# Softmax maxima of a head pair: turned first and split behind the transpose, with a reordered second block

## The chip, the cores and the metric

The kernel runs on one core of a Trainium2 chip. The metric is the time of one execution on the device in microseconds (us), median of several runs. One further execution is profiled; durations, waits and stretches below come from that one.

## The reference, cut to what matters

Two blocks of a transformer run one after the other over x of 8 sequences, 512 tokens and 256 features, with 16 heads of 16. The first has a bias on its scores; the second, `_L1_cond_ref`, masks the keys:

```
qkv = (x @ qkv_w).reshape(b, n, 3, H, D)
scores = jnp.einsum('bhnd,bhmd->bhnm', q, k) * scale
scores = jnp.where(mask, scores, -jnp.inf)
attn = jax.nn.softmax(scores, axis=-1)
out = jnp.einsum('bhnm,bhmd->bhnd', attn, v)
attn_out = out @ proj_w + proj_b
x = x + gate_msa[:, None, :] * _modulate(_layernorm(attn_out), shift_msa, scale_msa)
mlp_out = _mlp(x, fc1_w, fc1_b, fc2_w, fc2_b)
x = x + gate_mlp[:, None, :] * _modulate(_layernorm(mlp_out), shift_mlp, scale_mlp)
```

The mask of the second block leaves only keys among the last 128 tokens of each sequence. The kernel finds that out on the chip, from a flag, and then takes a short form of the second block; with these inputs it always does.

## The kernel before

A pass is one sequence in one block: passes 0 to 7 are the first block, 8 to 15 the second (`B` is 8, `N` 16). Each engine has its own program, written out as a loop over passes (`turn`), and waits on semaphores. Products outside the attention are cut into pieces: `v`, `qk` (queries and keys, four), `t1`, `t3`, `t2` (transposes), `wout`, `up` (eight) and `down` (four token tiles of eight chunks each). Pieces share three PSUM banks in a fixed round. While TensorE does the attention of pass n, it does the front of pass n + 1 and the back of pass n - 1 between.

In the short form (`short(n)`) a turn has 12 steps, p = 0 to 11. Tables set which pieces stand where: `HEADS` at the slots k = 3p, 3p + 1, 3p + 2, and `HEADS_DOWN` which of the 32 chunks of `down` stand at a slot. The heads go in 8 pairs, q = 0 to 7. For each pair:

- TensorE, step q + 2: `pair_scores_of` (L905) makes the scores, queries by keys, of both heads into the two `score` banks.
- DVE: `peaks_of` takes the maxima of every query (L1414), 8 columns for 2 heads and 4 token tiles; then a rounded high part (L1419) and the low rest (L1421) into `split_peak`, 16 columns.
- TensorE: `turn_peaks` (L912) transposes these into a corner of score bank 0, 16 rows of 128.
- DVE: `take_peaks` (L1429) copies them negated to `peaks`. The next `pair_scores_of` waits for it, as it overwrites the bank.
- ACT: `load_peaks` (L1113) issues a transfer of `peaks` into four rows of `q_rows` below the query rows, against which `k_rows` holds ones.
- TensorE, step q + 3: `turned_scores_of` (L924) makes the scores again, keys by queries, with the maxima subtracted by the extra rows. It waits for that transfer.
- ACT: `head_exp` (L1107), the exponentials, behind `load_peaks` of the next pair in its program. Then for every four heads, at steps 5, 7, 9, 11: `attend_heads` (L934), ACT's copy of its result (L1127), `heads_to_tokens` (L942), and DVE's division (L1437, L1439).

The order on TensorE within a step is: pair scores, slots 3p and 3p + 1, the values product, turned maxima, turned scores, slot 3p + 2, head outputs to tokens. At step 2 DVE adds the residual of the pass before (`add_tile`, L1268) or, at pass 8, applies the norm (`first_norm`, L1220); the `t2` transposes (L835) wait for it. On SP's queue, a short turn starts with the load of a residual if it is the first, and `load_few` loads the next pass's query and key rows of a group once `turned_scores_of` has used the old ones. ACT's gelu ("hidden", L1072) frees the bank of an `up` piece; gelu and exponential are in different tables, and a change between them costs a table load on ACT.

## Time and profile before

| what | value |
| --- | --- |
| median of 3 runs | 1460.7 us (1453.96 to 1461.02) |
| profiled execution, its own time | 1457.03 us |
| its span, first to last instruction | 1455.2 us |
| mean granted TensorE clock | 0.978 |
| busy: TensorE, DVE, ACT, POOL | 90%, 55%, 53%, 52% |
| second block, first pair scores to last | 900 to 1395 us |
| the eight turns of the second block | 893 to 1405 us, 62 to 66 us each |

Times are us from the first instruction. A granted clock of 1.00 is 2.4 GHz, and 0.5 is 1.2 GHz. "[1.89 <-DVE x_res L1268]" behind an instruction means that its engine sat idle for 1.89 us and that this DVE result released it. In the trace each fp32 chunk of `down` is two matmul records.

### The profile page before, as it was taken

Reading aid. Unit: us, or ns where it says so; the run is one execution under the profiler, and the core shown is the slowest. Engines: PE = TensorE matmul, PEld = TensorE weight load, DVE = VectorE, ACT = ScalarE, POOL = GpSimd, SP = SyncE. Lnnn points to the kernel's source line nnn. Section 1 sums busy time; section 2 is a strip of 40 time slices with the busy share of each in tenths; the row PEclk is TensorE's granted clock in tenths of the full one; section 3 lists DMA queues with packets and bytes.
Section 4 is the critical chain, followed back from the end, with each engine's and each line's share of the span. In section 5 each row is a group of like instructions: output and inputs, shape, how many; then the busy total and the mean of one; then the engine's idle time right before and its main releaser. Section 6 shows DMA issues by size and latency. Waiting matters only on the chain. (4 is left out here: it accounts for less than half of the span.)

```text
span 1455.2 us, 24552 instructions
## 1 busy us (share of the span) xinstructions
PE 1309.6 (90%) x8789; PEld 1004.0 (69%) x8789; DVE 803.2 (55%) x2240; ACT 770.5 (53%) x1262; POOL 757.1 (52%) x939
## 2 busy tenths in 40 slices
PE   4898999999999999999999997989888898988777
PEld 3676777777777777777777775666666666665556
DVE  3766645645646656656645643464655556454452
ACT  3565665665665765665655752544544353453522
POOL 3788876776776776776776761020413222140323
PEclk9999999999999999999999998999999999999988
DMA  8432222223213213213213215353424242433100
GB/s 258 130 127 57 71 84 72 73 75 83 74 64 89 75 58 88 78 55 88 79 54 110 92 41 164 113 152 108 151 67 145 61 155 93 123 116 86 45 2 29
DMA packets 98259, 133.98 MB, mean 92 GB/s; under 512 B 16802, under 2 KB 51498, under 8 KB 98130
## 3 DMA queue, kind: packets, MB, share of 16 engines
q1 hardware_dynamic: 96850, 131.80, 30.3%
q8 instruction: 73, 1.20, 0.3%
q10 hardware_dynamic: 1280, 0.53, 0.2%
q14 instruction: 56, 0.46, 0.1%
HBM read 72.64 MB, written 58.75 MB: 90 GB/s over the span
## 5 line engine op out<-in xcount | busy, mean ns | idle before, releaser
L617 POOL TENSOR_SCALAR shifted<-shifted,row_max 128x512 f32<-128x512 f32 x512 | 360.6, 719 | 220.1 <-DVE row_max L1380 218.2
L1380 DVE CUSTOM_DVE_ANT_0 shifted<-score,bias 128x512 f32<-128x512 f32 x512 | 332.7, 687 | 255.4 <-PE score L855 165.6
L1091 ACT ACTIVATE probs<-turned 128x512 f32<-128x512 f32 x512 | 278.2, 596 | 211.4 <-PE turned L867 209.8
L867 PE MATMUL turned<-ident,shifted 128*128 128x128 f32 x2048 | 270.0, 275 | 6.8 <-POOL shifted L617 6.0
L867 PEld LDWEIGHTS turned<-ident,shifted 128*128 128x128 f32 x2048 | 233.6, 141 | 55.6 <-issue 26.6
L783 PE MATMUL dense<-w_down,hidden 128*128 128x256 f32 x1024 | 253.3, 383 | 0.8 <-ACT hidden L1072 0.8
L610 POOL TENSOR_SCALAR bias<-dist,scale 128x1024 f32<-128x1024 f32 x192 | 220.0, 1146 | 13.6 <-DMA down_bias<-in_L_cond_b 13.6
L855 PE MATMUL score<-k_rows,q_rows 97*128 97x512 f32 x512 | 205.2, 456 | 22.1 <-DVE row_max L1380 10.1
L783 PEld LDWEIGHTS dense<-w_down,hidden 128*128 128x128 f32 x1024 | 185.6, 191 | 32.6 <-issue 9.6
L763 PE MATMUL dense<-feat_m,w_up 128*128 128x512 f32 x768 | 188.4, 400 | 3.5 <-ACT hidden L1072 1.8
L763 PEld LDWEIGHTS dense<-feat_m,w_up 128*128 128x128 f32 x768 | 144.3, 192 | 37.1 <-ACT hidden L1072 5.3
L855 PEld LDWEIGHTS score<-k_rows,q_rows 97*128 97x128 f32 x512 | 92.1, 190 | 65.0 <-DVE row_max L1380 51.5
L882 PE MATMUL pv<-probs,v_ext 128*32 128x256 f32 x2048 | 123.8, 382 | 0.8 <-DVE attn L1405 0.8
L631 POOL CAST mask_colf<-mask_col 128x4 f32<-128x4 uint8 x8 | 1.5, 188 | 234.7 <-PE pv L934 224.8
L1107 ACT ACTIVATE probs<-turned 128x512 f32<-128x512 f32 x128 | 69.5, 595 | 92.7 <-PE turned L924 61.8
L1072 ACT ACTIVATE hidden<-dense,up_bias 128x512 f32<-128x512 f32 x128 | 86.4, 688 | 54.2 <-PE dense L763 53.8
L763 PE MATMUL dense<-feat_a,w_qkv 128*128 128x512 f32 x384 | 109.0, 427 | 2.8 <-DVE feat_a L1334 2.8
L1414 DVE TENSOR_REDUCE row_max<-score 128x8 f32<-128x1024 f32 x64 | 78.1, 1221 | 36.5 <-PE score L905 36.5
L882 PEld LDWEIGHTS pv<-probs,v_ext 128*32 128x32 f32 x2048 | 60.2, 109 | 54.0 <-issue 17.7
L763 PEld LDWEIGHTS dense<-feat_a,w_qkv 128*128 128x128 f32 x384 | 73.7, 204 | 16.9 <-issue 3.2
L1059 ACT ACTIVATE qk_high<-dense 128x512 fp32r<-128x512 f32 x64 | 38.2, 597 | 77.1 <-PE dense L763 77.1
L1080 ACT ACTIVATE bias<-dist,scale 128x1024 f32<-128x1024 f32 x64 | 73.6, 1151 | 0.0
(138 smaller groups left out, 1497.3 us busy)
## 6 DMA issues: line engine op xcount, KB each, us to landing
qk_rows<-qk_high SPq DMA_DIRECT2D x128, 256.0 KB
q_rows<-qk_rows SPq DMA_DIRECT2D x64, 384.0 KB
qk_rows<-qk_low SPq DMA_DIRECT2D x64, 256.0 KB
k_rows<-qk_rows SPq DMA_DIRECT2D x68, 192.0 KB
x_in_t<-in_x SPq DMA_DIRECT2D x8, 512.0 KB, 3.8
x_res<-in_x SPq DMA_DIRECT2D x8, 512.0 KB, 5.5
x_mid<-x_norm SPq DMA_DIRECT2D x8, 512.0 KB, 3.3
x_in_t<-x_mid SPq DMA_DIRECT2D x8, 512.0 KB, 3.9
```

The source lines that it names most:

```text
L610: pool.tensor_scalar(bias[:, u % 2, :, :], dist[:, 2 * half:2 * half + 2, :], scale[:, h:h + 1], 0.0, ALU.mult, ALU.add).then_inc(s["bias_ ...
L617: ins = pool.tensor_scalar(shifted[:, u % 3, i, :], shifted[:, u % 3, i, :], -1.0, row_max[:, t % 6:t % 6 + 1], ALU.mult, ALU.add)
L763: mm = pe.matmul(out_ap, left, right, start=(i == 0), stop=(i == len(terms) - 1))
L783: mm = pe.matmul(bank_of(piece, m)[:, 0:D], hidden[:, c, P * i:P * i + P], w_down[:, c, :], start=(c == 0), stop=(c == FCH - 1))
L855: pe.matmul(score_bank[t % 2], q_rows[0:KROWS, g % 2, j // 2, q0:q0 + P], k_rows[0:KROWS, g % 2, j // 2, j % 2, :], start=True, stop=True) ...
L867: mm = pe.transpose(turned_bank[z % 2][:, HALF * kk + P * i:HALF * kk + P * i + P], shifted[:, u % 3, i, P * kt:P * kt + P], ident[:, :])
L882: mm = pe.matmul(pv_bank[SLOT * j:SLOT * j + SLOT, 0:HALF], v_ext[:, kt, HG * (gq // 2) + j, :], probs[:, (4 * gq + j) % RING, kt, :], sta ...
L1072: act.activation(hidden[:, i, :], bank[:, :], ACT.Gelu_apprx_tanh if m < B else ACT.Gelu, bias=up_bias[:, i:i + 1]).then_inc(used(piece, m ...
L1080: act.activation(bias[:, u % 2, :, :], dist[:, 2 * half:2 * half + 2, :], ACT.Copy, scale=scale[:, h:h + 1]).then_inc(s["act_bias_ready"], 1)
L1091: act.activation(probs[:, u % RING, 2 * pair:2 * pair + 2, :], turned_bank[z % 2][:, :].rearrange("p (a c) -> p a c", a=2), ACT.Exp)\
L1380: dve.tensor_tensor_reduce(shifted[:, u % 3, i, :], score_bank[t % 2], bias[:, u % 2, i, :], 1.0, 3.0e38, ALU.add, ALU.min, row_max[:, t % ...
L1414: dve.tensor_reduce(row_max[:, :].rearrange("p (a t) -> p t a", a=2), pair_scores, mybir.AxisListType.X, ALU.max).then_inc(s["peak_ready"], 1)
```

## The change

`split_peak` is gone. The 8 columns of maxima are transposed as they are (`turn_peaks` reads `row_max`), and DVE splits them behind the transpose: the high part negated and rounded, then in a second operation the rest, both reading the bank. ACT issues one transfer for the high rows when they are there (`peak_high`) and one for the low rows (`peaks_ready`); `peaks_loaded` counts 32 a pair. The rows in `q_rows` are ordered by part and then by head. On TensorE, the turned scores of the pair before now stand ahead of the turned maxima. On DVE, the residual's adds (or the norm at pass 8) at step 2 stand ahead of the pieces of that step's first slot. `HEADS_DOWN` moves chunks from slots 17, 20 and 26 to the slots ahead of them. The load of the first block's last residual moves on SP from the first short turn to the end of the turn before, ahead of the load of that turn's last group.

```diff
--- before.py
+++ after.py
@@ -70,8 +70,8 @@
              10: [("up", 0), ("up", 1), ("up", 2), ("up", 3)], 13: [("up", 4), ("up", 5), ("up", 6), ("up", 7)],
              19: [("down", 0)], 23: [("down", 1)], 28: [("down", 2)], 35: [("down", 3)]}
     HEAD_STEPS = H // 2 + 4
-    HEADS_DOWN = {16: (0, 4), 17: (4, 6), 19: (6, 9), 20: (9, 11), 22: (11, 14), 23: (14, 16), 25: (16, 19),
-                  26: (19, 21), 28: (21, 24), 29: (24, 25), 31: (25, 28), 34: (28, 29), 35: (29, 32)}
+    HEADS_DOWN = {16: (0, 6), 19: (6, 10), 20: (10, 11), 22: (11, 14), 23: (14, 16), 25: (16, 20), 26: (20, 21),
+                  28: (21, 24), 29: (24, 25), 31: (25, 28), 34: (28, 29), 35: (29, 32)}
 
     ANY = {0: [("v", 0), ("v", 1)], 1: [("t3", 0), ("t3", 1)], 2: [("v", 2), ("v", 3)], 3: [("t1", 0), ("t1", 1)],
            4: [("wout", 0)], 5: [("wout", 1)], 6: [("wout", 2)], 7: [("wout", 3)], 9: [("qk", 0)],
@@ -192,8 +192,7 @@
         hidden = sb("hidden", [P, FCH, L])
         feat_tmp = hidden[:, FCH - DC:FCH, :]
         row_max = sb("row_max", [P, 2 * TT])
-        split_peak = sb("split_peak", [P, 4 * TT], F32R)
-        peaks = sb("peaks", [4 * TT, P], F32R)
+        peaks = sb("peaks", [2 * TT, 2, P], F32R)
         minus_mean = sb("minus_mean", [P, TT])
         norm_shift = sb("norm_shift", [P, TT])
         stats = sb("stats", [P, 2, TT, 6])
@@ -245,7 +244,7 @@
                  "stats_ready0", "stats_ready1", "mean_ready0", "mean_ready1", "var_ready0", "var_ready1",
                  "rstd_ready0", "rstd_ready1", "norm_ready0", "norm_ready1", "bias_added", "mid_ready",
                  "res_ready0", "res_ready1", "scaled", "y_ready", "y_stored", "scale_step", "row_ones", "peak_high",
-                 "split_ready", "peak_turned", "peaks_ready", "peaks_loaded", "mean_minus", "norm_shift_ready", "normed",
+                 "peak_turned", "peaks_ready", "peaks_loaded", "mean_minus", "norm_shift_ready", "normed",
                  "y_scaled", "y_done", "last_ready", "tile_stats0", "tile_stats1", "tile_mean0", "tile_mean1", "tile_var0",
                  "tile_var1", "tile_rstd0", "tile_rstd1")
         s = {name: sem(name) for name in names}
@@ -467,7 +466,7 @@
                 sp.dma_start(flags, early_flag[:, :]).then_inc(s["flag_stored"], 16)
                 for a in range(2):
                     for x in range(2):
-                        at = PEAK_AT + 2 * a + x
+                        at = PEAK_AT + a + 2 * x
                         sp.dma_start(k_rows[at:at + 1, :, :, a, :].bitcast(F32),
                                      q_rows[MASK_AT:KROWS, 0:2, :, :].bitcast(F32)).then_inc(s["row_ones"], 16)
 
@@ -475,8 +474,6 @@
                 sp.wait_ge(s["halves_stored1"], STORED * (n + 1))
                 sp.sem_inc(s["base_free"], 1)
                 if n == B:
-                    sp.wait_ge(s["y_ready"], B - 1)
-                    load_res(B - 1)
                     sp.wait_ge(s["scores_used"], TILES * B)
                     load(raw_out[1], d["L1_cond_proj_w"].rearrange("(c p) n -> p c n", p=P), "wout_loaded")
                     load(raw_up[1], d["L1_cond_fc1_w"].rearrange("(c p) n -> p c n", p=P), "wup_loaded")
@@ -527,7 +524,8 @@
                     if n == 1:
                         sp.wait_ge(s["mod_stored"], 16)
                         sp.wait_ge(s["row_ones"], 64)
-                    load_res(n - 1)
+                    if n != B:
+                        load_res(n - 1)
                     if n - 1 >= B:
                         load_mod(n - 1)
                 if n == B - 1:
@@ -552,6 +550,9 @@
                     load_group(n + 1, 0)
                     if n > 0:
                         store_y(n - 1)
+                    if n == B - 1:
+
+                        load_res(n)
                     load_group(n + 1, 1)
                     return
                 if n + 1 < N:
@@ -908,8 +909,8 @@
                 mm.then_inc(s["scores_ready"], 2 * TT)
 
             def turn_peaks(n, q):
-                pe.wait_ge(s["split_ready"], H // 2 * (n - B) + q + 1)
-                pe.transpose(score_bank[0][0:4 * TT, 0:P], split_peak[:, :].bitcast(F32), ident[:, :])\
+                pe.wait_ge(s["peak_ready"], H // 2 * (n - B) + q + 1)
+                pe.transpose(score_bank[0][0:2 * TT, 0:P], row_max[:, :], ident[:, :])\
                     .then_inc(s["peak_turned"], 1)
 
             def turned_scores_of(n, q):
@@ -917,7 +918,7 @@
                 g, pair = q // 2, q % 2
                 if n == B and q == 0:
                     pe.wait_ge(s["row_ones"], 64)
-                pe.wait_ge(s["peaks_loaded"], 16 * (H // 2 * (n - B) + q + 1))
+                pe.wait_ge(s["peaks_loaded"], 32 * (H // 2 * (n - B) + q + 1))
                 for a in range(2):
                     h = 2 * q + a
                     pe.wait_ge(s["probs_ready"], TILES * n + (TT * (h - 1) if n > B or h > 0 else 0))
@@ -985,10 +986,10 @@
                                 down_chunks(n - 1, *HEADS_DOWN[k])
                         if attended:
                             attend_heads(n, (p - 5) // 2)
+                        if 3 <= p < 3 + H // 2:
+                            turned_scores_of(n, p - 3)
                         if 2 <= p < 2 + H // 2:
                             turn_peaks(n, p - 2)
-                        if 3 <= p < 3 + H // 2:
-                            turned_scores_of(n, p - 3)
                         for piece, m in pieces(HEADS, 3 * p + 2, n):
                             dense(piece, m)
                         if 3 * p + 2 in HEADS_DOWN:
@@ -1109,9 +1110,10 @@
 
             def load_peaks(n, q):
                 g, pair = q // 2, q % 2
-                act.wait_ge(s["peaks_ready"], H // 2 * (n - B) + q + 1)
-                act.dma_start(q_rows[PEAK_AT:ALL_ROWS, g, pair, :].bitcast(F32), peaks[:, :].bitcast(F32))\
-                    .then_inc(s["peaks_loaded"], 16)
+                for x, made in enumerate(("peak_high", "peaks_ready")):
+                    act.wait_ge(s[made], H // 2 * (n - B) + q + 1)
+                    act.dma_start(q_rows[PEAK_AT + 2 * x:PEAK_AT + 2 * x + 2, g, pair, :].bitcast(F32),
+                                  peaks[:, x, :].bitcast(F32)).then_inc(s["peaks_loaded"], 16)
 
             def normalize(m):
                 act.wait_ge(s["norm_shift_ready"], m - B + 1)
@@ -1409,25 +1411,20 @@
 
             def peaks_of(n, q):
 
-                count = H // 2 * (n - B) + q + 1
                 dve.wait_ge(s["scores_ready"], TILES * n + 2 * TT * (q + 1))
                 dve.tensor_reduce(row_max[:, :].rearrange("p (a t) -> p t a", a=2), pair_scores,
                                   mybir.AxisListType.X, ALU.max).then_inc(s["peak_ready"], 1)
-                dve.wait_ge(s["peak_ready"], count)
-                peak = row_max[:, :].rearrange("p (a t) -> p a t", a=2)
-                parts = split_peak[:, :].rearrange("p (a x t) -> p a x t", a=2, x=2)
-                dve.tensor_copy(parts[:, :, 0, :], peak).then_inc(s["peak_high"], 1)
-                dve.wait_ge(s["peak_high"], count)
-                dve.tensor_tensor(parts[:, :, 1, :], peak, parts[:, :, 0, :].bitcast(F32), ALU.subtract)\
-                    .then_inc(s["split_ready"], 1)
 
             def take_peaks(n, q):
                 count = H // 2 * (n - B) + q
                 dve.wait_ge(s["peak_turned"], count + 1)
                 if count > 0:
-                    dve.wait_ge(s["peaks_loaded"], 16 * count)
-                dve.tensor_scalar(peaks[:, :], score_bank[0][0:4 * TT, 0:P], -1.0, None, ALU.mult)\
-                    .then_inc(s["peaks_ready"], 1)
+                    dve.wait_ge(s["peaks_loaded"], 32 * count)
+                turned = score_bank[0][0:2 * TT, 0:P]
+                dve.tensor_scalar(peaks[:, 0, :], turned, -1.0, None, ALU.mult).then_inc(s["peak_high"], 1)
+                dve.wait_ge(s["peak_high"], count + 1)
+                dve.scalar_tensor_tensor(out=peaks[:, 1, :], in0=turned, scalar=-1.0, in1=peaks[:, 0, :].bitcast(F32),
+                                         op0=ALU.mult, op1=ALU.subtract).then_inc(s["peaks_ready"], 1)
 
             def divide_heads(n, g):
                 dve.wait_ge(s["token_ready"], GQ * n + 2 * g + 2)
@@ -1491,14 +1488,14 @@
             def turn(n):
                 if short(n):
                     for p in range(HEAD_STEPS):
-                        for piece, m in pieces(HEADS, 3 * p, n):
-                            dense(piece, m)
                         if p == 2:
                             if n == B:
                                 first_norm("norm", 1, n - 1)
                             else:
                                 for t in range(TT):
                                     add_tile(n - 1, 0, t)
+                        for piece, m in pieces(HEADS, 3 * p, n):
+                            dense(piece, m)
                         if 2 <= p < 2 + H // 2:
                             peaks_of(n, p - 2)
                         for piece, m in pieces(HEADS, 3 * p + 1, n):
```

TensorE at steps 3 to 5 of pass 9, from the turned maxima of pair 1 on, before:

```order
L912 MATMUL score<-ident,split_peak 16x128
L924 MATMUL turned<-q_rows,k_rows 128x512 x2
L905 MATMUL score<-k_rows,q_rows 128x256 x4
L763 MATMUL dense<-feat_m,w_up 128x512 x24
L912 MATMUL score<-ident,split_peak 16x128
L924 MATMUL turned<-q_rows,k_rows 128x512 x2
L905 MATMUL score<-k_rows,q_rows 128x256 x4
L783 MATMUL dense<-w_down,hidden 128x256 x4
L934 MATMUL pv<-probs,v_ext 32x512 x4
L912 MATMUL score<-ident,split_peak 16x128
L924 MATMUL turned<-q_rows,k_rows 128x512 x2
L783 MATMUL dense<-w_down,hidden 128x256 x2
```

and now:

```order
L925 MATMUL turned<-q_rows,k_rows 128x512 x2
L913 MATMUL score<-ident,row_max 8x128
L906 MATMUL score<-k_rows,q_rows 128x256 x4
L764 MATMUL dense<-feat_m,w_up 128x512 x24
L925 MATMUL turned<-q_rows,k_rows 128x512 x2
L913 MATMUL score<-ident,row_max 8x128
L906 MATMUL score<-k_rows,q_rows 128x256 x4
L784 MATMUL dense<-w_down,hidden 128x256 x6
L935 MATMUL pv<-probs,v_ext 32x512 x4
L925 MATMUL turned<-q_rows,k_rows 128x512 x2
L913 MATMUL score<-ident,row_max 8x128
```

The turned scores (`turned`) stand ahead of the turned maxima (the transpose into `score`), which now stand right ahead of the next pair scores; all six chunks of `down` stand ahead of the values product (`pv<-probs,v_ext`).

TensorE at steps 9 to 11 of the same pass, around the turned maxima of the last pair, before:

```order
L905 MATMUL score<-k_rows,q_rows 128x256 x4
L783 MATMUL dense<-w_down,hidden 128x256 x3
L934 MATMUL pv<-probs,v_ext 32x512 x4
L912 MATMUL score<-ident,split_peak 16x128
L924 MATMUL turned<-q_rows,k_rows 128x512 x2
L783 MATMUL dense<-w_down,hidden 128x256
L942 MATMUL pv<-ident,head_out 128x128 x4
L783 MATMUL dense<-w_down,hidden 128x256 x3
L924 MATMUL turned<-q_rows,k_rows 128x512 x2
L783 MATMUL dense<-w_down,hidden 128x256
L934 MATMUL pv<-probs,v_ext 32x512 x4
```

and now:

```order
L784 MATMUL dense<-w_down,hidden 128x256 x3
L935 MATMUL pv<-probs,v_ext 32x512 x4
L925 MATMUL turned<-q_rows,k_rows 128x512 x2
L913 MATMUL score<-ident,row_max 8x128
L784 MATMUL dense<-w_down,hidden 128x256
L943 MATMUL pv<-ident,head_out 128x128 x4
L784 MATMUL dense<-w_down,hidden 128x256 x3
L925 MATMUL turned<-q_rows,k_rows 128x512 x2
L784 MATMUL dense<-w_down,hidden 128x256
L935 MATMUL pv<-probs,v_ext 32x512 x4
```

Between the last turned maxima and the last turned scores, the turned scores of pair 6 no longer stand.

DVE at step 2 of the same pass, before:

```order
L1341 SCALAR_TENSOR_TENSOR qk_low<-dense,qk_high 128x512 x3
L1268 SCALAR_TENSOR_TENSOR shifted<-dist,rstd,shifted 128x256 x4
L1414 TENSOR_REDUCE row_max<-score 128x4x2
L1419 CAST split_peak<-row_max 128x2x4
L1421 TENSOR_TENSOR split_peak<-row_max,split_peak 128x2x4
L1337 TENSOR_TENSOR feat_m<-dense,feat_m 128x512 x2
L1429 TENSOR_SCALAR peaks<-score 16x128
L1341 SCALAR_TENSOR_TENSOR qk_low<-dense,qk_high 128x512
```

and now:

```order
L1343 SCALAR_TENSOR_TENSOR qk_low<-dense,qk_high 128x512 x2
L1270 SCALAR_TENSOR_TENSOR shifted<-dist,rstd,shifted 128x256 x4
L1343 SCALAR_TENSOR_TENSOR qk_low<-dense,qk_high 128x512
L1415 TENSOR_REDUCE row_max<-score 128x4x2
L1339 TENSOR_TENSOR feat_m<-dense,feat_m 128x512 x2
L1424 TENSOR_SCALAR peaks<-score 8x128
L1426 SCALAR_TENSOR_TENSOR peaks<-score,peaks 8x128
L1343 SCALAR_TENSOR_TENSOR qk_low<-dense,qk_high 128x512
```

The four adds of the residual (`shifted<-dist,rstd,shifted`) stand ahead of the third low part of queries and keys; cast and subtraction of the maxima are gone, and a second operation on `peaks` follows the first.

## Rows read from the trace of the kernel before

**Rows 1.** Stretches of us: busy PE, PEld, DVE, ACT, POOL; granted clock, DMA share, GB/s.

```profile
956.00:1019.00 63.00, 54.63 (x297) 40.67 (x296) 35.85 (x78) 29.08 (x44) 9.25 (x13) 1.00 0.51 151
...
1149.00:1213.00 64.00, 56.15 (x296) 41.70 (x296) 35.40 (x82) 29.64 (x47) 16.18 (x19) 0.97 0.36 115
```

**Rows 2.** Time line of TensorE, pass 9 then 12: start, us, instruction, [idle before].

```profile
973.93 1.64 PE L763 MATMUL dense<-feat_a,w_qkv 128*128 128x512 f32 x6
...
1164.17 1.98 PE L835 MATMUL dense<-ident,x_res 128*128 128x128 f32 x8 [1.89 <-DVE x_res L1268]
1166.81 0.38 PE L912 MATMUL score<-ident,split_peak 128*16 128x128 f32 x1 [0.66 <-DVE split_peak L1421]
1166.84 2.71 PE L763 MATMUL dense<-feat_a,w_qkv 128*128 128x512 f32 x6
...
1175.36 0.27 PE L912 MATMUL score<-ident,split_peak 128*16 128x128 f32 x1
...
1176.09 0.71 PE L905 MATMUL score<-k_rows,q_rows 97*128 97x256 f32 x4
...
1181.17 1.67 PE L763 MATMUL dense<-feat_m,w_up 128*128 128x512 f32 x6 [0.22 <-ACT hidden L1072]
1182.68 0.27 PE L912 MATMUL score<-ident,split_peak 128*16 128x128 f32 x1
...
1186.65 1.06 PE L934 MATMUL pv<-probs,v_ext 128*32 128x512 f32 x8 [0.86 <-ACT probs L1107]
...
1189.71 0.72 PE L905 MATMUL score<-k_rows,q_rows 97*128 97x256 f32 x4
...
1192.43 0.28 PE L912 MATMUL score<-ident,split_peak 128*16 128x128 f32 x1 [0.70 <-DVE split_peak L1421]
...
1193.75 0.83 PE L905 MATMUL score<-k_rows,q_rows 97*128 97x256 f32 x4
...
1202.00 0.28 PE L912 MATMUL score<-ident,split_peak 128*16 128x128 f32 x1 [0.99 <-DVE split_peak L1421]
...
1203.31 0.81 PE L905 MATMUL score<-k_rows,q_rows 97*128 97x256 f32 x4
...
1206.35 0.28 PE L912 MATMUL score<-ident,split_peak 128*16 128x128 f32 x1
...
1209.00 0.82 PE L924 MATMUL turned<-q_rows,k_rows 101*128 101x512 f32 x2
...
1210.84 1.06 PE L934 MATMUL pv<-probs,v_ext 128*32 128x512 f32 x8 [0.59 <-ACT probs L1107]
```

**Rows 3.** Time line of DVE, the same turn of pass 12.

```profile
1162.94 0.69 DVE L1341 SCALAR_TENSOR_TENSOR qk_low<-dense,qk_high 128x512 fp32r<-128x512 f32 x1 [0.97 <-ACT qk_high L1059]
1163.55 1.66 DVE L1268 SCALAR_TENSOR_TENSOR x_res<-dist,rstd,x_res 128x256 f32<-128x256 f32 x4
1165.13 1.22 DVE L1414 TENSOR_REDUCE row_max<-score 128x8 f32<-128x1024 f32 x1
...
1197.23 0.28 DVE L1429 TENSOR_SCALAR peaks<-score 16x128 fp32r<-16x128 f32 x1 [0.99 <-DMA q_rows<-peaks]
...
1206.67 0.28 DVE L1429 TENSOR_SCALAR peaks<-score 16x128 fp32r<-16x128 f32 x1
```

**Rows 4.** Time line of ACT and its queue (ACTq), the same turn.

```profile
1183.30 0.64 ACTq L1113 DMA_DIRECT2D q_rows<-peaks  x1
...
1185.31 1.08 ACT L1107 ACTIVATE probs<-turned 128x512 f32<-128x512 f32 x2
...
1193.41 0.64 ACTq L1113 DMA_DIRECT2D q_rows<-peaks  x1
...
1206.98 0.64 ACTq L1113 DMA_DIRECT2D q_rows<-peaks  x1
```

**Rows 5.** Time line of TensorE at the entry of the second block.

```profile
895.31 1.02 PE L763 MATMUL dense<-w_out,feat_m 128*128 128x256 f32 x6 [2.12 <-DVE x_res L1350]
```

**Rows 6.** DMA issues by line: count, KB each, median us to landing.

```profile
x_res<-in_x SPq DMA_DIRECT2D x8, 512.0 KB, 5.5
```

## The prediction

> **What bounds the kernel now.** I read the granted clock by stretches first, then the time line of TensorE over one turn of the second block (a turn is one sequence: 16 heads in 8 pairs), and last the lines of the engines that TensorE waits for. The change touches only the eight turns of the second block (about 893 to 1405 us) and one load ahead of them. A turn takes some 64 us, in which TensorE has work in 56 [rows 1]: it sets the pace, and what counts is which waits of TensorE go and come. In the turn shown [rows 2] it waits 1.89 us for the residual rows (DVE L1268), 0.66 for the maxima of pair 0, 0.22 at the last "up" piece (for ACT), 0.86 at the first product with the values (for ACT's exponentials), 0.70 and 0.99 for the maxima of pairs 4 and 6, and 0.59 before the last heads. The reader should see that ahead of pairs 1 to 3 nothing waits for maxima: the order of before hides them behind the "up" products. I call the turning of a pair's maxima (L912) T, and the scores matmuls of the next pair (L905) S.
>
> **Costs that the rows give.** From T to the DVE's take of the turned maxima 0.32, which itself takes 0.28, and 0.63 from T to ACT's issue of the transfer [rows 2, 3, 4]. An issue holds ACT for 0.64 us, and the exponentials start behind it: 2.63 behind T where the table must be loaded (1182.68 to 1185.31) [rows 2, 4]. The turned scores of pair 7 run 2.02 us behind the issue without a wait (1206.98 to 1209.00), so a transfer is usable by then; beside SP's loads it took 3.82 (1193.41 to 1197.23) [rows 2, 3, 4].
>
> **1. The move of the adds on DVE (step 2).** DVE idles 0.97 before the low half of a query/key piece, does it, and only then adds the residual (4 tiles in 1.66) [rows 3]. Now the adds come first, and TensorE's wait for them shrinks by about 1.6 of 1.89. The reduce starts about 0.95 earlier. Cast and subtraction are gone between reduce and T: before, T stood 1.68 behind the reduce's start (1165.13 to 1166.81), of which 1.22 is the reduce; now about 1.27 [rows 2, 3]. So T of pair 0 comes 1.35 earlier. S of pair 1 gains less: the DVE still does the two low halves of the norm first (about 1.3 us), then both takes; S is ready at about 1167.35. With a full clock the piece between takes 1.64 (pass 9), so S would have come at 1168.3 [rows 2]. **Gain 0.9 a turn.**
>
> **2. The order of T and the turned scores, and the second take.** The turned scores of the pair before (0.54 us of TensorE's time) now stand ahead of T. Behind T, S overwrites the bank, so it waits for both takes: 0.32 + 0.28, a step of 0.03, and a second operation of the same 128 columns, taken at 0.28, make 0.95 with the release. For pairs 1 and 2 nothing stands between T and S. Before it was 0.73 from T to S (1175.36 to 1176.09), with the turned scores inside [rows 2]; now it is 0.54 + 0.95 = 1.5. **Loss 0.8 at pair 1.** Pair 2 has the same, but there ACT's lateness covers it, as follows.
>
> **3. The second issue on ACT.** ACT still issues the maxima of pair q before it takes the exponentials of pair q - 1. T is 0.55 later, and the second issue takes 0.64 more, so exponentials and what follows them come 1.2 later seen from the turned scores. At pair 1 the "hidden" activations follow and free the bank of the last "up" piece, at which TensorE already waits [rows 2, 4]. Seen from pair 1 that piece is 1.2 later, of which 0.8 was counted: **loss 0.4.** At pair 2, T is 0.55 later and the exponentials another 0.64; the first values product stood 3.97 behind T (1182.68 to 1186.65) and now stands about 4.6, so **loss 1.2**, S's wait of 0.85 and the two down chunks moved ahead of it (step 16 now has six, step 17 none) lying in that same time. What hides them is ACT; were ACT faster, they would stand there themselves.
>
> **4. Pairs 3 to 6.** From the values product to S of pair 4 it was 3.06 (1186.65 to 1189.71). Now it is 1.0 + 0.54 + 0.95 = 2.5, as the two chunks are already done: **gain 0.55.** The waits of 0.70 and 0.99 for maxima go, since the chunks and the turned scores (some 2.9 us) cover the reduce; but with one chunk left in steps 20 and 26, S waits about 0.45 behind T, and the values products of steps 7 and 9 wait 0.2 for the later exponentials. From S to S I get 3.95 instead of 4.04 (1189.71 to 1193.75), 0.1 more for the next and 0.4 less for the third: **gain 0.4** [rows 2].
>
> **5. Pair 7.** Its turned scores stood 2.65 behind T (1206.35 to 1209.00), without a wait [rows 2]. Now only one chunk, the turning of head outputs and three chunks lie between, about 2.1, and the second transfer is issued at 1.27 behind T. I take 1.8 for it to be usable, a little under the 2.02 that bounds it from above: it arrives at 3.1 to 3.2, and TensorE waits 1.0. From S of pair 7 to the last values product it was 7.53 (1203.31 to 1210.84). Now T comes at 4.0 (3.04 as before, 0.2 for later exponentials, 0.2 for the turned scores of pair 6 and these themselves 0.54), the turned scores 3.15 later, and the product 1.84 behind them as before: 9.0, **loss 1.5**. The Trainium skill, "DMA: Bandwidth & Descriptors", section "Anatomy of one DMA", gives a fixed cost of about 2.0 us a transfer whatever its size (a fit for another issuing path); by that the last wait would be 1.2 and the sum 1.6 us higher over eight turns. Two small transfers in place of one save nothing there by that rule, and the row of 2.02 leaves room for it.
>
> **The sum.** A steady turn: -0.9 + 0.8 + 0.4 + 1.2 - 0.55 - 0.4 + 1.5 = +2.05. Six of them: +12.3. The last turn has no query/key pieces, so step 1 gives 0.1 instead of 0.9: +2.9. The first turn waits for the norm's rstd and not for the moved piece, and takes 0.3 more for the second take: +3.2; but the load of the residual is now issued before the block, ahead of the last group. Before, it held DVE and so TensorE for 2.12 us [rows 5]; it lands 5.5 behind its issue [rows 6], which moves ahead of that group's load and of the branch, so I take the wait as gone whole, and TensorE is 2.1 earlier: +1.1. The group load that it puts back by one issue on SP is first used at pair 2 of the block, and nothing waits for SP here. Cast and subtraction also free DVE of about 0.4 us a pair, hidden beside TensorE but for what is counted. Sum +16 us on the profiled 1457.0: 1473. The median of the three runs is 3.7 above the profiled execution (they lie at 1454.0 and twice near 1461), so a median would come at 1473 to 1476.7; I give **1475**.
>
> Bounds of the unknown prices: the second take from nothing to 0.69 (a whole 512-column operation [rows 3]); the second issue from nothing to 0.64; the landing from its issue alone, 0.64, to 3.82. They move a turn by -2.1 to +2.
>
> **Rivals.**
> - **The second issue costs ACT nothing** (not slower). If ACT's queue takes both issues in the time of one, TensorE loses 0.6 less at pair 1, 0.3 at pair 2, 0.2 at each of the two values products, and 0.64 at pair 7: 2 us a turn, and with eight turns 1457. For it: the issue can run beside an activation. Against it: the exponentials start right behind the issue's end in every row [rows 4]. It decides from the point at which exponentials start less than 2.8 us behind T with a table load.
> - **The clock pays it back.** The turn shown has a granted clock of 0.97 where pass 9 has 1.00, and the piece behind T of pair 0 takes 2.71 instead of 1.64, so some 1.1 us is lost to a stretch at 1.2 GHz behind the 1.89 and 0.66 of waiting [rows 1, 2]. If such a stretch vanishes from each of the eight turns, 9 us come back: 1464. Against it: new waits of the same size arise at pairs 2 and 7. The Trainium skill, "TensorE: Matmul & The Clock Gate", says in "What's actually happening" that the gate follows how busy the array has recently been; by that alone the place of the stretches moves with the waits, either way.
> - **The second transfer lands late beside SP's loads.** Pairs 2, 4 and 6 are issued with SP's group loads, and now within a third of a microsecond after them. If the second needs 3.82 from its own issue, the turned scores of these pairs wait 0.5 to 0.9 more each: about 1.8 a turn, 1486. I take only 0.2, since the delay looks like one backlog that both stand behind.
> - All gains at once, with no stall behind T: about 1445.
>
> **Chances.** Forecast 0.55, issue 0.12, clock 0.15, late landing 0.13, all gains 0.05. The range takes in the first four with their bounds: 1456 to 1488. Runs can tell about 0.5 per cent. Faster by more than that 0.08 (the last, and part of the clock), within it 0.20 (issue, half of the clock), slower 0.72.
>
> **What would show it.** TensorE idle before S of pairs 2 and 3, released by the new DVE take, some 0.9 us each; none before T of pairs 4 and 6; before the residual's transposes about 0.3 instead of 1.89; two ACT issues of 0.64 in a row; turned scores of pair 7 waiting 1 us; no 2.12 at the entry. The forecast is wrong if S follows T by under 0.8 us at pairs 1 and 2, or if the turn, from values transposes to the next, is not longer than before.

## The result, and the profile after

| | before | changed |
| --- | --- | --- |
| median, 9 runs each | 1460.7 us (1453.96 to 1462.6) | 1467.72 us (1464.27 to 1472.03) |
| ratio, 95% interval | 1 | 1.0056 (1.004 to 1.0072) |
| profiled execution, its own time | 1457.03 us | 1464.27 us |
| span, mean granted clock | 1455.2 us, 0.978 | 1462.5 us, 0.985 |

The change is slower by 0.56%, about half of what was forecast (1475). Stretches of the changed kernel, columns as in [rows 1]:

```profile
956.00:1019.00 63.00, 53.76 (x279) 39.39 (x281) 33.77 (x69) 27.38 (x43) 7.66 (x11) 0.97 0.48 143
1019.00:1083.00 64.00, 55.52 (x294) 40.29 (x294) 32.68 (x74) 28.89 (x47) 16.16 (x19) 1.00 0.37 114
1149.00:1213.00 64.00, 54.85 (x292) 39.54 (x290) 32.68 (x74) 28.49 (x46) 16.14 (x19) 1.00 0.37 115
```

From 1019 us to 1343 every such stretch has a granted clock of 1.00 (2.4 GHz), where before each had 0.97, as the second of [rows 1]. The first one goes the other way, 1.00 before and 0.97 now: pass 9 holds a stretch at half clock that it did not have. TensorE lost time to waits and got some back from the clock. The time line of TensorE in pass 12, answering to [rows 2] (T is L913 here, S L906, turned scores L925):

```profile
1165.35 1.86 PE L836 MATMUL dense<-ident,x_res 128*128 128x128 f32 x8 [0.24 <-DVE x_res L1270]
1168.18 0.27 PE L913 MATMUL score<-ident,row_max 128*8 128x128 f32 x1 [0.97 <-DVE row_max L1415]
1168.20 1.63 PE L764 MATMUL dense<-feat_a,w_qkv 128*128 128x512 f32 x6
1169.87 0.74 PE L906 MATMUL score<-k_rows,q_rows 97*128 97x256 f32 x4
...
1176.55 0.27 PE L913 MATMUL score<-ident,row_max 128*8 128x128 f32 x1
1177.60 0.71 PE L906 MATMUL score<-k_rows,q_rows 97*128 97x256 f32 x4 [0.78 <-DVE peaks L1426]
...
1183.76 1.67 PE L764 MATMUL dense<-feat_m,w_up 128*128 128x512 f32 x6 [1.32 <-ACT hidden L1073]
...
1185.78 0.28 PE L913 MATMUL score<-ident,row_max 128*8 128x128 f32 x1
1186.74 0.74 PE L906 MATMUL score<-k_rows,q_rows 97*128 97x256 f32 x4 [0.68 <-DVE peaks L1426]
1187.32 2.75 PE L784 MATMUL dense<-w_down,hidden 128*128 128x256 f32 x12
1190.40 1.07 PE L935 MATMUL pv<-probs,v_ext 128*32 128x512 f32 x8 [0.33 <-ACT probs L1108]
1192.17 0.70 PE L925 MATMUL turned<-q_rows,k_rows 101*128 101x512 f32 x2 [0.71 <-issue]
...
1193.76 0.71 PE L906 MATMUL score<-k_rows,q_rows 97*128 97x256 f32 x4 [0.34 <-DVE peaks L1426]
...
1201.25 0.70 PE L925 MATMUL turned<-q_rows,k_rows 101*128 101x512 f32 x2 [0.52 <-issue]
...
1206.85 0.74 PE L906 MATMUL score<-k_rows,q_rows 97*128 97x256 f32 x4 [0.25 <-DVE peaks L1426]
...
1210.70 0.28 PE L913 MATMUL score<-ident,row_max 128*8 128x128 f32 x1
...
1213.76 0.71 PE L925 MATMUL turned<-q_rows,k_rows 101*128 101x512 f32 x2 [0.61 <-DMA q_rows<-peaks]
...
1215.49 1.07 PE L935 MATMUL pv<-probs,v_ext 128*32 128x512 f32 x8 [0.59 <-ACT probs L1108]
```

The residual's wait went from 1.89 to 0.24, the one ahead of T of pair 0 from 0.66 to 0.97, the waits of 0.70 and 0.99 for maxima are gone, and the piece behind T of pair 0 takes 1.63 instead of 2.71. New are the waits of S for DVE's second operation (0.78, 0.68, 0.34, 0.25), 1.32 instead of 0.22 at the last "up" piece, and 0.61 before the turned scores of pair 7. Of the 0.71 and 0.52 ahead of the turned scores of pairs 2 and 4 the forecast had almost nothing. DVE (compare [rows 3]) takes twice behind T:

```profile
1164.72 1.66 DVE L1270 SCALAR_TENSOR_TENSOR x_res<-dist,rstd,x_res 128x256 f32<-128x256 f32 x4
...
1166.91 1.22 DVE L1415 TENSOR_REDUCE row_max<-score 128x8 f32<-128x1024 f32 x1
...
1176.86 0.28 DVE L1424 TENSOR_SCALAR peaks<-score 8x128 fp32r<-8x128 f32 x1 [3.55 <-PE score L913]
...
1177.18 0.28 DVE L1426 SCALAR_TENSOR_TENSOR peaks<-score,peaks 8x128 fp32r<-8x128 f32 x1
```

ACT and its queue (compare [rows 4]) show two issues in a row and the exponentials behind both:

```profile
1177.17 2.04 ACTq L1115 DMA_DIRECT2D q_rows<-peaks  x2
1179.33 1.28 ACT L1108 ACT_TABLE_LOAD   x1 [2.49 <-issue]
...
1186.40 1.28 ACTq L1115 DMA_DIRECT2D q_rows<-peaks  x2
1187.77 1.28 ACT L1108 ACT_TABLE_LOAD   x1 [1.61 <-issue]
1189.06 1.09 ACT L1108 ACTIVATE probs<-turned 128x512 f32<-128x512 f32 x2
```

For pair 2 the exponentials start 3.28 behind T (1185.78 to 1189.06), where it was 2.63. At the entry of the block the wait of [rows 5] is gone, and the queries and keys run at the full clock; first the changed kernel, then before:

```profile
891.51 3.07 PE L764 MATMUL dense<-w_out,feat_m 128*128 128x256 f32 x24
894.42 2.96 PE L764 MATMUL dense<-feat_a,w_qkv 128*128 128x512 f32 x12
```

```profile
896.13 4.49 PE L763 MATMUL dense<-feat_a,w_qkv 128*128 128x512 f32 x12
```

**A turn in six stretches.** T of pair q is the turning of its maxima, S of pair q are its scores matmuls. One turn is not enough to compare by. I took the start times of six events of TensorE from the time line in each of the six steady turns (passes 9 to 14): the turn's first transposes (`dense<-ident,attn`), S of pairs 1 and 2, the first values product, S of pairs 4 and 7, the last values product. Means in us; from the last one to the next turn it is 4.62 everywhere. The kernels are those of the experiments below. Each has one profile, so how far these means scatter from run to run is not known.

| kernel | ratio | to S 1 | to S 2 | to 1st values | to S 4 | to S 7 | to last values | turn |
| --- | --- | --- | --- | --- | --- | --- | --- | --- |
| before | 1 | 17.33 | 6.80 | 10.54 | 3.85 | 13.71 | 7.78 | 64.62 |
| changed | 1.0056 | 15.56 | 7.73 | 12.36 | 3.16 | 13.12 | 8.97 | 65.52 |
| forecast, difference | | -0.9 | +0.8 | +1.6 | -0.55 | -0.4 | +1.5 | +2.05 |
| measured, difference | | -1.77 | +0.93 | +1.82 | -0.69 | -0.59 | +1.19 | +0.90 |
| e1 | 0.9978 | 17.63 | 7.14 | 10.56 | 3.40 | 13.73 | 7.86 | 64.93 |
| e2 | 0.9987 | 15.81 | 6.83 | 10.54 | 5.18 | 13.73 | 7.90 | 64.61 |
| e3 | 0.9929 | 16.29 | 7.27 | 11.00 | 3.46 | 13.07 | 8.16 | 63.88 |
| e4 | 1.002 | 15.75 | 7.25 | 12.11 | 4.71 | 13.24 | 8.22 | 65.89 |
| e5 | 1.0042 | 15.89 | 7.38 | 12.62 | 2.49 | 13.27 | 8.98 | 65.26 |
| e6 | 0.9871 | 15.73 | 7.19 | 11.02 | 2.30 | 12.65 | 8.30 | 61.79 |
| e7 | 1.0029 | 15.80 | 7.65 | 12.18 | 2.62 | 13.15 | 9.10 | 65.11 |
| e8 | 1.01 | 16.91 | 7.56 | 12.31 | 2.69 | 13.19 | 9.26 | 66.53 |
| e9 | 0.9965 | 16.39 | 7.42 | 12.12 | 2.38 | 12.65 | 8.32 | 63.90 |
| e10 | 0.9888 | 15.96 | 6.96 | 10.54 | 2.80 | 13.67 | 7.92 | 62.46 |
| e11 | 0.9858 | 16.30 | 7.32 | 10.44 | 2.30 | 12.57 | 8.22 | 61.76 |
| e12 | 1.0041 | 15.80 | 7.67 | 10.75 | 4.48 | 13.80 | 8.85 | 65.96 |

The six turns one by one are 63.27, 63.87, 66.51, 63.76, 64.33, 66.00 before and 66.60, 64.70, 66.28, 65.57, 63.76, 66.21 now. Two of them are shorter than before, and 3.33 of the 5.4 us that all six are longer lie in pass 9. (The first turn takes 70.74 before and the last 60.99, so the "62 to 66 us each" in the table of the kernel before is too narrow.)

In before, passes 10, 12 and 13 run the piece behind T of pair 0 partly at half clock (2.91, 2.71 and 2.89 for the six matmuls), and pair 2 does not wait for its transfer. Passes 11 and 14 run the piece at full clock (1.65) and wait 1.23 and 1.01 at pair 2. Pass 9 has neither; its first stretch is 0.7 longer than in these two. e3 alternates in the same way: half clock in passes 9, 11 and 13, waits of 2.04, 2.47 and 1.90 at pair 2 in 10, 12 and 14. So it is the turn with a short first stretch that meets the wait at pair 2. My reading, argued and not tested by itself, is that its maxima are issued closer behind SP's loads.

### The profile page after: what moved, and what is told of

Same layout as the page of the kernel before. It is cut to its first block and busy times, and to the rows that moved or that the text cites. A ratio compares the mean times of both kernels' runs of the same rounds, so it can differ in the third digit from the quotient of the medians.

```text
span 1462.5 us, 24552 instructions
## 1 busy us (share of the span) xinstructions
PE 1308.8 (89%) x8789; PEld 995.2 (68%) x8789; DVE 787.5 (54%) x2176; ACT 769.6 (53%) x1262; POOL 754.6 (52%) x939
## 5 line engine op out<-in xcount | busy, mean ns | idle before, releaser
L784 PE MATMUL dense<-w_down,hidden 128*128 128x256 f32 x1024 | 250.2, 381 | 0.8 <-ACT hidden L1073 0.8
L784 PEld LDWEIGHTS dense<-w_down,hidden 128*128 128x128 f32 x1024 | 182.2, 190 | 33.1 <-issue 9.6
L764 PE MATMUL dense<-feat_a,w_qkv 128*128 128x512 f32 x384 | 104.3, 413 | 2.8 <-DVE feat_a L1336 2.8
L1424 DVE TENSOR_SCALAR peaks<-score 8x128 fp32r<-8x128 f32 x64 | 17.8, 278 | 147.1 <-PE score L913 147.1
```

Source lines behind the costliest of these rows:

```text
L764: mm = pe.matmul(out_ap, left, right, start=(i == 0), stop=(i == len(terms) - 1))
L784: mm = pe.matmul(bank_of(piece, m)[:, 0:D], hidden[:, c, P * i:P * i + P], w_down[:, c, :], start=(c == 0), stop=(c == FCH - 1))
```

## Experiments: the parts alone

Ratios are to the kernel before, run again beside each kernel, with 95% intervals.

**e1: the early load alone.** The load of the first block's last residual moves as in the change.

> The kernel before with the load of the first block's last residual issued one turn earlier on SP, nothing else. Theory (each wait of TensorE counts for itself): the wait of 2.1 us at the entry of the second block goes, ratio about 0.9985. Rival (clock): the stretches at half clock at the entry go as well, 3 to 4 us in all, ratio 0.9975. If it were hidden elsewhere: 1.000.

1455.74 us, 0.9978 (0.996 to 0.9996): about 3 us, the size of the 2.12 of [rows 5] and what it brings. The interval takes in the wait alone (0.9985) and the wait with its half clock (0.9975); in the profile the first turn is 4.45 shorter (70.74 to 66.29), which speaks for the second.

**e2: and the adds first on DVE.**

```diff
                     for p in range(HEAD_STEPS):
-                        for piece, m in pieces(HEADS, 3 * p, n):
-                            dense(piece, m)
                         if p == 2:
...
+                        for piece, m in pieces(HEADS, 3 * p, n):
+                            dense(piece, m)
```

> As e1, and DVE adds the residual ahead of the query/key piece at step 2. Theory of waits alone: 0.9 to 1.3 us less in each of six turns beyond e1, ratio about 0.993 to 0.994 with e1's part. Rival (clock pays as well): the half-clock stretch behind that wait, 1.1 to 1.7 us in five turns, goes too, the granted clock of passes 10 to 14 reads 1.00, and the ratio is about 0.989.

1456.33 us, 0.9987 (0.9971 to 1.0003): nothing more than e1, where the two theories had 0.993 to 0.994 and 0.989. The table shows where it went. Up to S of pair 1 a turn is 1.82 us shorter than in e1 (17.63 to 15.81), and from the first values product to S of pair 4 it is 1.78 longer (3.40 to 5.18). TensorE in e2, pass 12, at T of pair 0 and at the turned scores of pair 2:

```profile
1164.41 0.28 PE L913 MATMUL score<-ident,split_peak 128*16 128x128 f32 x1 [1.38 <-DVE split_peak L1422]
...
1186.04 1.19 PE L925 MATMUL turned<-q_rows,k_rows 101*128 101x512 f32 x2 [1.58 <-issue]
```

The turned scores of pair 2 wait 1.58 for the maxima and then run at half the clock (1.19 for two matmuls, 0.70 elsewhere). Before has this in two of its six turns; its pass 11, which I had not read, on TensorE, and the issues ahead of it on ACT and on SP:

```profile
1121.60 1.19 PE L924 MATMUL turned<-q_rows,k_rows 101*128 101x512 f32 x2 [1.23 <-issue]
```

```profile
1115.74 0.64 ACTq L1113 DMA_DIRECT2D q_rows<-peaks  x1
```

```profile
1111.96 0.51 SPq L340 DMA_DIRECT2D x_res<-x_mid  x1
1112.51 1.58 SPq L343 DMA_DIRECT2D dist<-mod_rows  x1
```

5.86 us from issue to use: SP's two loads of 512 KB each were issued 3.8 and 3.2 us ahead of it.

**e3: the new order on TensorE and the chunk table too, with the old split and one transfer.** Against the changed kernel this takes back the split alone:

```diff
-                pe.wait_ge(s["peak_ready"], H // 2 * (n - B) + q + 1)
-                pe.transpose(score_bank[0][0:2 * TT, 0:P], row_max[:, :], ident[:, :])\
+                pe.wait_ge(s["split_ready"], H // 2 * (n - B) + q + 1)
+                pe.transpose(score_bank[0][0:4 * TT, 0:P], split_peak[:, :].bitcast(F32), ident[:, :])\
...
-                for x, made in enumerate(("peak_high", "peaks_ready")):
...
+                act.wait_ge(s["peaks_ready"], H // 2 * (n - B) + q + 1)
+                act.dma_start(q_rows[PEAK_AT:ALL_ROWS, g, pair, :].bitcast(F32), peaks[:, :].bitcast(F32))\
+                    .then_inc(s["peaks_loaded"], 16)
```

> The changed kernel with the old split: cast and subtraction ahead of the transpose, one take, one transfer; load, adds, TensorE order and chunk table as changed. Theory (second take and second issue are what costs): against the changed kernel TensorE's waits before the pair scores shrink from 0.7 to 0.8 to some 0.4, ACT's exponentials come 0.9 earlier seen from the turned maxima, and pair 7 waits 0.3 less or more: 1.5 to 2 us a turn, so 12 to 16 us less than the changed kernel, ratio to before about 0.995 to 0.997. Rival (the TensorE order itself costs): little changes against the changed kernel, ratio 1.003 to 1.006.

1449.19 us, 0.9929 (0.9904 to 0.9953): faster than before, and than the 0.995 to 0.997 that I expected. All of the loss, and more, is in the split with its two transfers: 1.27% of the time of before.

**e4: that split with the old order and the old table.**

```diff
-    HEADS_DOWN = {16: (0, 6), 19: (6, 10), 20: (10, 11), 22: (11, 14), 23: (14, 16), 25: (16, 20), 26: (20, 21),
+    HEADS_DOWN = {16: (0, 4), 17: (4, 6), 19: (6, 9), 20: (9, 11), 22: (11, 14), 23: (14, 16), 25: (16, 19),
...
-                        if 3 <= p < 3 + H // 2:
-                            turned_scores_of(n, p - 3)
                         if 2 <= p < 2 + H // 2:
                             turn_peaks(n, p - 2)
+                        if 3 <= p < 3 + H // 2:
+                            turned_scores_of(n, p - 3)
```

> The changed kernel with the old TensorE order (turned maxima ahead of the turned scores) and the old chunk table; split behind the transpose, two transfers, load and adds as changed. Theory: against e2 the waits of 0.7 and 1.0 before the maxima of pairs 4 and 6 shrink by 0.4 each, and 0.25 at pairs 1 and 2, 0.3 at ACT and 0.5 at pair 7 are lost: within 2 us a turn of nothing, ratio to e2 0.998 to 1.003. Rival (split is what costs): as slow as the changed kernel, 1.005.

1461.32 us, 1.002 (1.0004 to 1.0037). The parts don't add up. The split with its two transfers costs 0.33% over e2 in the old order and 1.27% over e3 in the new one; the new order gains 0.58% with one transfer and loses 0.36% with two. It puts T behind the turned scores and leaves less work between T of pair 7 and its use: time that a second issue needs. The last stretch of the table is 8.22 here and 8.97 in the changed kernel. That is part of an answer only. The fourth stretch goes the other way (4.71 here, 3.16 there), so that the steady turns are no shorter here (65.89 and 65.52), and the eight turns take 524.6 us in both profiles. The profiles don't show where the 0.36% lies.

**e8: the changed kernel with the adds behind the piece again,** the edit of e2 undone.

> The changed kernel with DVE's adds again behind the query/key piece. Theory: TensorE waits 1.9 us for the residual again, T of pair 0 comes 0.95 later, and the half-clock stretch returns in most turns: 1 to 2 us a turn, ratio to before 1.010 to 1.014. Rival (the gain is eaten at pair 2's landing, as e2 against e1): ratio 1.005 to 1.007.

1472.37 us, 1.01 (1.0082 to 1.0117). Here the move of the adds is worth 0.44%, some 6 us, while alone (e2) it was worth nothing. In the changed kernel pair 2's maxima are issued later in the turn and meet less of SP's loads: the adds take 1.35 off the first stretch (16.91 to 15.56) and put 0.47 on the fourth (2.69 to 3.16), where in e2 they put 1.78.

## Experiments: what makes the second transfer dear

**e5: e3 with its one transfer issued as two.** DVE's work and all orders are as in e3.

```diff
-                act.dma_start(q_rows[PEAK_AT:ALL_ROWS, g, pair, :].bitcast(F32), peaks[:, :].bitcast(F32))\
-                    .then_inc(s["peaks_loaded"], 16)
+                for a in range(2):
+                    act.dma_start(q_rows[PEAK_AT + 2 * a:PEAK_AT + 2 * a + 2, g, pair, :].bitcast(F32),
+                                  peaks[2 * TT * a:2 * TT * a + 2 * TT, :].bitcast(F32)).then_inc(s["peaks_loaded"], 16)
```

> e3 (old split, new order) with its one transfer of the maxima issued as two, one per head; DVE and TensorE unchanged. Theory (the second issue of 0.64 us on ACT is the main price of the change): exponentials 0.64 later in every pair, TensorE later at the last up piece, at the first values product and before pair 7's turned scores, 1 to 1.5 us a turn, 8 to 12 us, ratio to before 0.999 to 1.001. Rival (the second take ahead of the pair scores is the price): within 3 us of e3, ratio 0.993 to 0.995.

1465.05 us, 1.0042 (1.0029 to 1.0055): 1.13% over e3, about 16 us for 64 further issues of 4 KB, where I expected 8 to 12. That is nearly all that lies between e3 and the changed kernel; the move of the split behind the transpose costs what is left, 0.14%, which the intervals don't tell from nothing.

The Trainium skill, "DMA: Bandwidth & Descriptors", section "Rules for kernel authors", says of two transfers to disjoint partition halves "Don't bother", since both use the same DMA engines. The runs agree that nothing is won, with 16 us as the price here; they show no cost of shared DMA engines, only that of the second issue and of its landing.

**e9: e3 with work on ACT in the place of the second issue.**

```diff
                     .then_inc(s["peaks_loaded"], 16)
+                for i in range(3):
+                    act.activation(idle_out[:, i, :], ident[:, 0:80], ACT.Copy)
```

> The version with the old split and one transfer (e3), with three copies of 80 columns on ACT behind each issue, into a tensor that nothing reads; they take ACT's time and touch no queue, as a second issue would take 0.64 us there. If the second issue costs what it does because ACT takes the exponentials and all behind them later (theory one), this loses what the two issues of e5 lost against e3, some 2 us a turn: ratio to before 1.003 to 1.005. If it costs because the turned scores wait for the later of two transfers (theory two), this loses nothing: 0.991 to 0.995. Between the two, the share of ACT's time can be read off.

1453.16 us, 0.9965 (0.9952 to 0.9977): 0.36% over e3, a third of what the issue costs, and the intervals of e3 and e9 touch. ACT of e9, then of e5, at pair 1 of pass 12:

```profile
1173.19 0.66 ACTq L1115 DMA_DIRECT2D q_rows<-peaks  x1
1173.90 0.59 ACT L1118 ACTIVATE idle_out<-ident 128x80 bf16<-128x80 f32 x3 [0.91 <-DVE peaks L1433]
1174.50 1.28 ACT L1109 ACT_TABLE_LOAD   x1
```

```profile
1178.75 1.28 ACTq L1115 DMA_DIRECT2D q_rows<-peaks  x2
1180.13 1.28 ACT L1108 ACT_TABLE_LOAD   x1 [1.59 <-issue]
```

Both put the table load about 0.6 us back. In the third stretch e9 loses 1.12 a turn against e3 and e5 1.62; over the first three stretches together both lose about 1.35. What differs most is the end of the turn, where the turned scores of pair 7 wait for their transfer: e9 +0.16, e5 +0.82. On the other side both win about 1 us in the fourth stretch (3.46 to 2.38 and 2.49); I put that down to the later issue, with which pair 2 is past SP's loads. The sum over a steady turn is nothing for e9 (63.88 to 63.90) and +1.38 for e5. So neither theory alone: ACT's time is the larger part of the loss up to the first values product and is paid back at pair 2, and the landing of the second transfer at pair 7 is not. What e9 costs in its profile lies outside the steady turns, 2.24 of it in the first turn (67.80 to 70.04) and 2.0 ahead of the block, where the profiles scatter as much.

**e12: the changed kernel with the exponentials ahead of both issues.**

```diff
-                        if 2 <= p < 2 + H // 2:
-                            load_peaks(n, p - 2)
                         if 3 <= p < 3 + H // 2:
                             for a in range(2):
                                 head_exp(n, 2 * (p - 3) + a)
+                        if 2 <= p < 2 + H // 2:
+                            load_peaks(n, p - 2)
```

> The changed kernel, with ACT taking the exponentials of the pair before ahead of both issues of a pair's maxima. The maxima wait for the issues, and the exponentials no longer do. If the price of the second issue is that exponentials and gelu stand 0.64 us further back (the waits of 1.3 us at the last up piece and 0.3 to 0.7 at the values products), those waits go back to what the one-transfer version shows and the ratio to before comes to 0.996 to 1.000. If it is the later landing of the second transfer, the turned scores now wait for it at most pairs and the ratio is 1.006 to 1.015. The filler run says a third of the price is ACT's time, by which I would expect about 1.001 if the transfers had slack.

1462.65 us, 1.0041 (1.0023 to 1.0059), which the intervals don't tell from the changed kernel's 1.0056; I expected about 1.001. The wait of 1.32 at the last "up" piece is gone and the third stretch 1.61 shorter; the fourth is 1.32 longer and the fifth 0.68. TensorE, pass 12:

```profile
1182.27 0.74 PE L906 MATMUL score<-k_rows,q_rows 97*128 97x256 f32 x4 [0.69 <-DVE peaks L1426]
...
1188.77 1.09 PE L925 MATMUL turned<-q_rows,k_rows 101*128 101x512 f32 x2 [2.17 <-issue]
...
1199.25 0.71 PE L925 MATMUL turned<-q_rows,k_rows 101*128 101x512 f32 x2 [1.00 <-issue]
```

What was saved at ACT is waited for at the next landing. I read it so: the waits stand in a row along one path, from T over DVE, ACT's queue and the transfer to the turned scores, beside SP's loads.

## Experiments: SP's loads out of the way

**e6: e3 with the two loads of 512 KB for the residual moved, in passes 9 to 14, behind the turn's last load of query and key rows.**

```diff
-                load_res(n)
-                load_mod(n)
+                late = B < n < N - 1
+                if not late:
+                    load_res(n)
+                    load_mod(n)
...
+                if late:
+                    load_res(n)
+                    load_mod(n)
```

> e3 with SP's loads of residual and modulation rows (1 MB) of passes 9 to 14 moved behind the last group load of the turn. Theory (pair 2's maxima stand behind these loads on the DMA engines, and TensorE then waits up to 2.5 us for them, which eats what the earlier adds gave): that wait is under 0.7 and 1.5 to 2 us a turn go, 9 to 12 us, ratio about 0.985 to 0.987. Rival (the group's own load holds them): no change against e3, ratio 0.993.

1439.68 us, 0.9871 (0.9855 to 0.9887), 0.6% faster than e3. In e3, pass 12, the turned scores of pair 2 wait; SP's issues ahead of them stand below:

```profile
1181.79 0.71 PE L925 MATMUL turned<-q_rows,k_rows 101*128 101x512 f32 x2 [2.47 <-issue]
```

```profile
1171.15 0.51 SPq L340 DMA_DIRECT2D shifted<-x_mid  x1
1171.70 1.47 SPq L343 DMA_DIRECT2D shifted<-mod_rows  x1
```

They were issued 3 us ahead of T of pair 2 (1174.28). In e6 the same pair does not wait, and the loads are issued 28 us behind its T (1174.15):

```profile
1179.13 0.73 PE L930 MATMUL turned<-q_rows,k_rows 101*128 101x512 f32 x2
```

```profile
1202.11 0.45 SPq L340 DMA_DIRECT2D shifted<-x_mid  x1
1202.61 0.49 SPq L343 DMA_DIRECT2D shifted<-mod_rows  x1
```

The fourth stretch is 2.30 in all six turns, and the granted clock is 1.00 in them, as here in pass 12 (columns as in [rows 1]):

```profile
1146.00:1208.00 62.00, 55.30 (x295) 40.32 (x296) 35.23 (x84) 29.98 (x48) 16.53 (x20) 1.00 0.38 121
```

**e7: the same move in the changed kernel.**

> The changed kernel with the same move of the loads. Theory: TensorE waits 0.6 to 0.8 for pair 2's maxima in the changed kernel, so 0.5 to 0.8 us a turn go, 3 to 5 us, ratio about 1.002 to 1.004. Rival (other waits take it): 1.0056 as the changed kernel.

1462.26 us, 1.0029 (1.0017 to 1.004). So the price of the new split with two transfers is no smaller without the two bulk loads: e7 over e6 is 1.6%, where the changed kernel over e3 is 1.27%, a difference within the intervals. The second transfer landing late beside these loads is not the main cost. The rival of the prediction spoke of SP's group loads (query and key rows), which stay where they are. Beside them the turned scores of pair 4 wait 0.18 to 0.79 in e7, and 0.24 to 0.66 in e6 with one transfer: the second adds little there too.

**e10: e2 with the same move,** old order, table and split.

> The kernel before with the early load of the residual, the adds first on DVE (as e2), and SP's large loads of passes 9 to 14 moved behind the turn's last load of query and key rows; the order on TensorE, the split and the single transfer as before. Theory: the adds gained nothing in e2 because the transfer of pair 2's maxima then stood behind those loads; with them away the gain of some 0.4 to 0.6 per cent appears, ratio 0.990 to 0.994, and what remains to e6 (0.987) is the order on TensorE with the chunk table. Rival: the gain was eaten at the turned maxima of pair 0 alone, which stay late here: 0.996 to 1.000.

1443.11 us, 0.9888 (0.9871 to 0.9905): 1% faster than e2, and the fourth stretch is back at 2.80. That confirms where the adds' gain had gone. It is a little more than I expected; the half clock at pair 2 goes with the wait. The move of the loads alone, without the adds, was not run.

**e11: e6 with the exponentials first,** the edit of e12.

> The best version so far (e6) with ACT taking the exponentials of the pair before ahead of the issue of a pair's maxima instead of behind it. Exponentials start up to 0.7 us earlier, the transfer up to 1.1 us later. If the exponentials bound the step (the waits at the values products and at the last up piece), it gains 0.3 to 0.6 us a turn: ratio 0.983 to 0.986. If the landing of the maxima bounds it, the turned scores wait for it at every pair: slower than e6 by 2 us a turn or more, 0.995 to 1.01.

1437.33 us, 0.9858 (0.9841 to 0.9875): the fastest, though not told from e6. The third stretch is 0.58 shorter. With one transfer and the bulk loads moved the later issue costs nothing, unlike in e12.

## Why the prediction was right, and its size too large

The sign, the range and the mechanism held: S waits for both takes, the exponentials stand behind two issues, pair 7 waits for its second transfer, and no wait is left before T of pairs 4 and 6. That the time lies in the range says little by itself, since 1456 to 1488 took in three rivals as well; the forecast's own 1475 was 14 us over before, and 7 were measured. By its steps, in us a steady turn:

- **Step 1, forecast -0.9, measured -1.77. This is the term that was mis-sized.** I reckoned the gain against a full clock ("S would have come at 1168.3"), while S stood at 1169.39. In passes 10, 12 and 13 of before, the stretch from the residual's transposes to S of pair 1 took 5.38, 5.22 and 5.36, in 9, 11 and 14 it took 4.15: 3.5 us over six turns for a half clock. In the changed kernel it is 4.52 in five of six. I had set this apart as the rival "The clock pays it back" with 0.15, and held against it that new waits of the same size arise. They arose, and the granted clock stayed at 1.00 in passes 10 to 14, while pass 9 fell to 0.97: part of that rival came true beside the forecast. The clock is only about half of the excess. Between turns at full clock on both sides the stretch went from 16.62 (passes 11 and 14 of before) to 15.33, a gain of 1.29: the residual's wait shrank by 1.65 as reckoned, and S of pair 1 came 0.3 earlier than the 1167.35 at which I had it ready (1169.87 in a turn that begins 2.84 later).
- **Step 2, +0.8, measured +0.93.** S follows T by 1.05 (1176.55 to 1177.60) where 0.95 was taken; DVE's second operation took 0.28 as taken.
- **Step 3, +1.6, measured +1.82.** The threshold of the rival that the issue costs nothing was 2.8 from T to the exponentials; it was 3.28. e9, +1.12 in this stretch, shows that time on ACT does most of this. The two issues of pair 1 took 1.88 to 2.04 in passes 10 to 12, where the stretch is 12.6 to 12.8, and 1.30 to 1.38 in the others, where it is 12.0 to 12.1 as forecast; that is the excess.
- **Step 4, -0.95 in both stretches, measured -1.28, but not for the reason given.** In turns without a landing wait the fourth stretch went from 2.80 to 2.62 only. Most of the mean's gain is that before lost 3 us there in passes 11 and 14 (5.81 and 5.68), to pair 2's landing. Pass 12, the turn I had read, shows none of that. In the changed kernel it lost up to 1.2.
- **Step 5, +1.5, measured +1.19.** Pair 7 waited 0.61, not 1.0. T to the turned scores was 3.06 (1210.70 to 1213.76); I had put the landing at 3.1 to 3.2, so that was right, and TensorE had 2.45 to do between and not the 2.1 that I took. From the second issue, 1.27 behind T, to the matmul that it released it is 1.79, as I took it and a little below the fixed cost of about 2.0 cited in the prediction. The wait of 0.61 lies below the 1.0 and the 1.2 that these gave.
- **The first turn, +1.1, measured -2.5** (70.74 to 68.25). The entry wait of 2.12 went as said; the half clock behind it went too (4.49 to 2.96 for the same twelve matmuls).
- **The last turn, +2.9, measured +2.3** (60.99 to 63.27).

The sum inside the eight turns is 6 x 0.90 - 2.5 + 2.3 = +5.2, where I had 16. Of the 11 us that are missing, 5.2 are step 1 in six turns and 3.6 the first turn. The profiled execution is 7.2 longer; the other 2 us lie outside the turns. The first block, in which nothing is changed but that load at its end, ends 1.4 later, and over all profiles its end scatters from 886.4 to 892.2 (e1). The medians differ by 7.0.

The traces hold more on how a transfer of ACT's queue is held up: its packets (20 for 8 KB) have a queue of their own. In us behind the issue:

| transfer | first packet | last packet | use |
| --- | --- | --- | --- |
| before, pass 12, pair 7: no other packets | 1.28 | 1.44 | 2.02 |
| e6, pass 12, pair 2: bulk loads moved, group load beside it | 2.29 | 2.57 | 4.36 |
| before, pass 11, pair 2 | 2.93 | 4.95 | 5.86 |
| e3, pass 12, pair 2 | 4.33 | 6.17 | 6.89 |

In e3, SP's queue moved 697 packets between the issue and the first of these 20, with the DMA engines busy throughout (the packets' time comes to 102.5% of 16 engines'). So most of the delay lies ahead of the first packet (3.0 of 4.9 us against pair 7), the rest between the packets, which take 1.8 us instead of 0.2. What stays open is why: the traces don't show whether the transfer stood ready in its queue meanwhile.

## What to carry to other kernels

A small transfer on the way from one engine to another costs its issue on the issuing engine, in front of everything queued there, and its landing. Count both, and don't make two transfers of one. Read several turns of a loop before costing one: the wait that matters can be in every third (here in passes 11 and 14 of six). When an edit on the path gains nothing, look for a wait that grew by the same amount further on: here it was a transfer behind another queue's bulk loads. Moving those gained 0.6 to 1.0% in the kernels with one transfer (e6, e10), more than the whole change cost, and 0.27% in the changed kernel (e7).
